# The residual add of a fused post-norm layer, moved ahead of the last unit of maxima on VectorE

## The reference, cut to what matters

```python
x = L0_attn_x                                   # (16, 512, 256)
x = _layernorm(x + _L0_attn_ref(x, Wqkv, bqkv, Wout, bout))
x = _layernorm(x + _L0_ffn_ref(x, W1, b1, W2, b2))
# inside the attention, per head and window:
scores = einsum(qb, kwin) * scale
attn = softmax(where(mask, scores, -1e30))
out = (attn @ v) ... ; return out @ Wout + bout
```

## Time and profile before

| | |
|---|---|
| median of 3 runs | 1079.29 us (1078.25 to 1079.56) |
| the profiled execution's own time | 1080.47 us |
| its span, first to last instruction | 1078.7 us |
| mean granted clock of TensorE | 0.969 |
| busy: PE, DVE, ACT, POOL | 996.8, 845.2, 620.2, 570.2 us |
| period of a pass (adds at 371.33 and 433.66 us) | 62.3 us |

### The profile page before, as it was taken

The page is one execution under the profiler, slowest core; times in us unless marked ns, Lnnn a source line. Parts: engine busy times, 40 slices in busy tenths (PEclk is TensorE's granted clock), DMA queues, the critical chain, the costliest instruction groups (busy, mean ns, idle before and its releaser), DMA issues.

```text
span 1078.7 us, 29877 instructions
## 1 busy us (share of the span) xinstructions
PE 996.8 (92%) x11270; PEld 782.0 (72%) x11270; DVE 845.2 (78%) x2966; ACT 620.2 (57%) x1273; POOL 570.2 (53%) x913
## 2 busy tenths in 40 slices
PE   6898999999999999999999999999999999999897
PEld 5675777777777777777767777786777778687677
DVE  3775888879788887978888787988878798887535
ACT  4244665746566574756657474765747475564632
POOL 3975356374655537465554646454464645445352
PEclk8577999999999999999999999999999999999999
DMA  9554336546354545626454652645365364435000
GB/s 222 64 82 72 57 57 95 81 74 94 55 91 66 96 70 81 99 43 97 66 96 63 94 87 49 100 65 96 56 100 80 57 96 68 73 52 81 22 21 20
DMA packets 57023, 81.90 MB, mean 76 GB/s; under 512 B 7712, under 2 KB 27696, under 8 KB 56880
## 3 DMA queue, kind: packets, MB, share of 16 engines
q1 hardware_dynamic: 56640, 79.60, 46.8%
q10 hardware_dynamic: 240, 0.39, 0.3%
HBM read 20.20 MB, written 8.39 MB: 26 GB/s over the span
## 4 chain that ended last, share of the span: by engine, by line
PE 61%; DVE 13%; ACT 12%; issue 6%; POOL 4%; DMA 2%; SPq 1%; DVEq 0%; POOLq 0%; ACTq 0%
PE shared L592 26%; PE shared L641 11%; PE st L549 8%; PE mx L567 6%; DVE mx L1061 6%; ACT probs L895 4%; PE shared L521 2%; ACT x L963 2%; ACT u L946 2%; DVE hid_lo L1147 2%; PE shared L654 2%; ACT oT_x1T_hi L969 2%; PE shared L612 1%; POOL probs L1285 1%; POOL probs L1289 1%
## 5 line engine op out<-in xcount | busy, mean ns | idle before, releaser
L1061 DVE CUSTOM_DVE_ANT_0 mx<-mx,band 128x384 f32<-128x384 f32 (+1 forms) x1024 | 478.9, 518 | 150.5 <-PE mx L567 145.4
L895 ACT ACTIVATE probs<-st 128x384 f32<-128x384 f32 (+1 forms) x768 | 365.1, 526 | 169.8 <-PE st L549 168.1
L1285 POOL TENSOR_SCALAR_AFFINE_SELECT probs<-probs 128x512 f32<-128x512 f32 (+1 forms) x256 | 127.8, 524 | 407.0 <-ACT probs L895 407.0
L567 PE MATMUL mx<-k_stack,q_stack 48*128 48x384 f32 (+1 forms) x1024 | 271.7, 347 | 8.5 <-DMA q_stack<-qk_lo 4.9
L549 PE MATMUL st<-q_stack,k_stack 50*128 50x384 f32 (+1 forms) x1024 | 245.1, 334 | 7.8 <-ACT probs L895 3.8
L549 PEld LDWEIGHTS st<-q_stack,k_stack 50*128 50x128 f32 x1024 | 167.7, 189 | 58.9 <-issue 29.8
L567 PEld LDWEIGHTS mx<-k_stack,q_stack 48*128 48x128 f32 x1024 | 171.8, 193 | 31.1 <-DVE rmax L1061 19.2
L641 PE MATMUL shared<-probs,v_aug 128*32 128x384 f32 (+1 forms) x2048 | 164.2, 444 | 9.4 <-POOL probs L1289 7.2
L1061 DVE DVE_READ_ACCUMULATOR2_ANT rmax<- 128x1 f32 x1024 | 144.9, 141 | 0.0
L592 PE MATMUL shared<-w2q,hid_hi 64*128 64x256 f32 x960 | 137.0, 289 | 0.0
L641 PEld LDWEIGHTS shared<-probs,v_aug 128*32 128x32 f32 x2048 | 90.5, 111 | 55.8 <-issue 17.7
(11 more groups left out here) (165 smaller groups left out, 1935.7 us busy)
## 6 DMA issues: line engine op xcount, KB each, us to landing
q_stack<-qk_hi SPq DMA_DIRECT2D x128, 128.0 KB, 4.0
k_stack<-qk_hi SPq DMA_DIRECT2D x126, 128.0 KB, 4.9
x_raw<-in_xT SPq DMA_DIRECT2D x16, 512.0 KB, 6.0
q_stack<-qk_lo SPq DMA_DIRECT2D x64, 128.0 KB, 5.6
y<-in_x SPq DMA_DIRECT2D x16, 512.0 KB, 6.3
out<-x SPq DMA_DIRECT2D x32, 256.0 KB, 2.4
k_stack<-qk_lo SPq DMA_DIRECT2D x63, 128.0 KB, 5.8
probs<-in_w2T SPq DMA_DIRECT2D x1, 1024.0 KB, 7.5
```

The source lines that it names most:

```text
L567: mm = pe.matmul(PMX[i % N_MAX][:, col:col + n], SQ[rows, hd, W * m:W * m + W], SK[rows, hd, k0:k0 + n], start=True, stop=True)
L895: act.activation(PR[:, v % 2, g // 2, lo:lo + n], PST[i % N_SCORE][:, 0:n], ACT.Exp, scale=SCALE) \
L1061: mx = dve.tensor_tensor_reduce(ps, ps, band, 1.0, -3e38, ALU.add, ALU.max, RMAX[:, g, m:m + 1])
L1285: pool.affine_select(out=pr_before, in_=pr_before, compare_op=ALU.is_ge, fill=0.0, base=0, pattern=[[0, n], [1, W]], channel_multiplier=-1)
```

## The change: what it does

A table `AHEAD` names the step `op`, with the number 1. `dve_order` now stops ahead of the last unit of maxima that is woven into such a step, emits every step still held back and then the step itself, and only then the last unit (with the negation that belongs to it). The other stages' orders come out as before. Stage 0 is now: unit 10, `op`, unit 11, negated maxima, then `ln1` 0 to 3. The programs of the other engines are not touched.

```diff
 LAG = {"ln1": 3, "ln2": 0, "qk": 0, "ut": 0, "ot": 1, "x1t": 0, "f1": 0, "op": 0, "f2": 0}
+AHEAD = {"op": 1}
 N_PAIRS = 2
...
-        for _, kind, i in woven:
-            if kind == "max":
-                out.append(("max", i))
-                maxima += 1
-                due(maxima)
+        units = [i for _, kind, i in woven if kind == "max"]
+        first = len(units) - min(AHEAD.get(step, 0), len(units))
+        for n, i in enumerate(units):
+            if n == first:
+                due(UNITS + 100)
+                out.append(("side", step))
+            out.append(("max", i))
+            maxima += 1
+            due(maxima)
+        if first < len(units):
+            continue
         after = late[-1][0] + 1 if late and name_of(late[-1][1]) == name_of(step) == "ln2" else 0
         late.append((max(maxima + LAG.get(name_of(step), 0), after), step))
         due(maxima)
```

## The result

The changed kernel is **slower**, by 0.7% in the ratio: 1088.83 us median (1085.7 to 1089.5, 4 runs) against 1078.77 (1077.79 to 1079.56, 4 runs of the kernel before), ratio 1.0069 with a 95% interval of 1.0048 to 1.009. The profiled executions took 1089.01 and 1080.47 us, spans 1087.3 and 1078.7: 8.6 us more.

A forecast was written before the change was run, and what follows sets the result against it. TensorE, busy 92%, was taken to bound the kernel together with a chain through VectorE. 13 x 0.58 + 0.2 + 0.41 = 8.1 us on 1080.47 gave 1088.6, less 1.2 for the median: 1087.4 us, range 1082.5 to 1093.0.

The forecast's parts named there:

- The add meets its own data: Stage 0, VectorE: the adds wait for the output projection's last matmul, putting VectorE's work back by 0.41 us per pass.
- Unit 11 read later, TensorE held: Stage 1's second maxima load waits for unit 11's bank, 0.94 us; half a load's length won back, TensorE 0.85 us late.
- What stays of it: After the projection: first x +0.42, copy of u +0.58, low keys branch 0.41; the latest counts, 0.58 us per pass.
- Nothing gained from the freed banks: Two PSUM banks come free 0.93 us sooner; gain nothing, at most 0.5 us in the last pass. Faster rival: chance 0.04.
- The sum: Whole kernel: 13 x 0.58 + 0.2 + 0.41 = 8.1 us slower.
- The load's idle time: Stage 1: TensorE's load of maxima would wait 0.9 us for VectorE's reading, 13 times.
- The pass of its own: The pass at 870.73, where TensorE came late already: only 0.2 us lost there.
- The last pass: No projection follows and ScalarE waits 2.00 us for GpSimd's part, so VectorE's 0.41 us counts.
- The rule of the Trainium skill that was weighed: TensorE pulls weight loads ahead of running matmuls; applied to the stalled load, the sum would be 1.2 us lower; not used.

The follow-up runs named there:

- late maxima run: The changed kernel with units 0 and 1 of stage 1's maxima moved on TensorE to the end of the first projection; 1086.15 us, ratio 1.0061.
- second run: The kernel before, VectorE's order untouched, but TensorE's second unit of maxima of stage 1 also waits until y is written; 1091.87 us, ratio 1.0108.
- late negation: Negation of the maxima moved behind the first two statistics: on the kernel before 1077.21 us, ratio 0.9976; on the changed kernel 1088.87 us, ratio 1.0074.
- one add ahead: Half of the change: one of the two adds ahead of unit 11, the other behind the negation; 1087.51 us, ratio 1.007 against the kernel before.

## Why the prediction was right

- **The add meets its own data.** Foreseen: 0.23 too early, adds at +0.04, VectorE 0.41 late. Shown: a wait of 0.26 ahead of the adds in 15 of 15 passes, and the statistics 0.45 late. The late maxima run gives this delay's price as 0.39 per pass when it stands alone.
- **Unit 11 read later, TensorE held.** Foreseen: the load 0.94 late, 0.85 behind that. Shown: 0.92 and, at the product's end (376.63 + 2.32 = 378.95, 6.46 behind the projection's last matmul, before 5.64), 0.82. That the 0.85 fits is in part luck, since it took half of a load's length between two values with no row for the half. That the stall alone costs time was shown by the second run, and that it is the branch that counts by the late negation, which gained nothing in the changed kernel.
- **What stays of it.** Foreseen 0.58 in 13 passes and 0.2 in one, found 0.60 as the mean of the 14. The product's end starts u, as written. The first x (377.75 - 372.49 = 5.26, before 4.79) and the load that waits for the low part of the keys (379.53 - 372.49 = 7.04, before 6.58) moved by less, as written, but by 0.47 and 0.46 and not by 0.42 and 0.41. The wait for the keys shrank from 0.60 to 0.23, foreseen 0.15.
- **Nothing gained from the freed banks.** The add's line shows nobody waiting for it after the change; before it was 0.5 us, once.
- **The sum.** 13 x 0.58 + 0.2 + 0.41 = 8.1 against 8.5 in the profiled executions. Term by term the errors are small and go both ways: 0.64 in each of the 13 passes, 0.11 in the one that was late already, 0.47 in the last (both below). The forecast of 1087.4 lies 1.4 under the median. The medians differ by 10.1, more than the ratio's interval (5.2 to 9.7 us) and the profiled executions (8.5) say: the four runs of the kernel before were low ones, its medians beside the later runs are 1080.1 to 1080.4, with single runs from 1076.5 to 1082.6. So the spread of 1078.25 to 1079.56 that the prediction counted with was too narrow.
- **What was sized a little wrong.** The load's idle time was said to be 0.9 us, 13 times. It is 0.73 to 0.96 in eleven passes and less in three, 0.65 in the pass shown, where the scores ahead of it came late as well; the load's distance from the projection (2.16) is the steady number.
- **The pass of its own** The earlier trace rows was late through a DMA. The chain of the kernel before has there:

```profile
864.95 5.61 DMA q_stack<-neg_maxT
```

Its adds start at 869.97 and the next ones at 932.83; those of the changed kernel in the same pass and the next are the two rows behind:

```profile
932.83 1.27 DVE L1117 TENSOR_TENSOR y<-shared,y 128x512 f32<-128x512 f32 x2
...
876.36 1.29 DVE L1124 TENSOR_TENSOR y<-shared,y 128x512 f32<-128x512 f32 x2 [0.25 <-PE shared L599]
...
939.33 1.29 DVE L1124 TENSOR_TENSOR y<-shared,y 128x512 f32<-128x512 f32 x2 [0.25 <-PE shared L599]
```

So this pass took 62.86 before and 62.97 after, and lost 0.11, foreseen 0.2. The 13 others lost (8.4 - 0.11) / 13 = 0.64 each. In the changed kernel no pass stands out: the load stands 2.16 behind the projection here too. That the stall hides such lateness in general was not tried.
- **The last pass**, foreseen 0.41. ScalarE's wait for GpSimd ahead of x, 2.00 before, grew by 0.47:

```profile
1007.52 1.09 ACT L970 ACTIVATE x<-y,ln_neg_mean_rstd,ln_rstd 128x256 f32<-128x256 f32 x2 [2.47 <-POOL ln_neg_mean_rstd L1364]
```

The rule of the Trainium skill that was weighed (TensorE: Matmul & The Clock Gate, Part 2: loads are pulled ahead) would have made the stall shorter by a load, if it held for a load that itself waits. In the run with the stall alone, the load and its matmul both start at 375.99, idle 1.04 before it. So the load that waits for the semaphore was not done during the wait; the rule's case, a load pulled ahead of running matmuls, is not this one.

## What to carry to other kernels

Before moving a step ahead of a unit of other work, ask two questions of the trace: is its input there at the new time (here it was 0.23 us too late, because the producer's own program has the overtaken unit ahead of the step's last matmuls), and who waits for the buffer that the overtaken unit frees (here TensorE, in the middle of another step). Here the move took nothing off the chain to the normalised x, since unit 11 only changed its place in it, and so it only added waits. What shortened that chain was taking a piece out of it that its end does not need, the negation, and even that paid only up to the next branch.

## What the runs showed of the hardware

A wait that blocks VectorE can cost more than the time it blocks. Behind a blocked wait of 0.27 us ahead of unit 11 the second negation's row was 0.48 long for 0.28, and the adds started 0.41 behind it, and 0.20 with nothing blocked, while the same extra instruction on a met semaphore changed nothing (62.33). With one add ahead, behind a blocked wait of 0.26, the same step took 0.18, so blocking alone does not explain it. Why this is so was not settled. The adds themselves took 686 ns at their earlier place and 676 at the old one, 685 in the version with the late negation; they ran beside other work there, and which of it slowed them was not tried.
